# A 4096-step LSTM inside a graph network kernel: the two waits of three VectorE instructions are named in the other order

## What is computed

```python
def step(carry, xp):
    h, c = carry
    gates = xp + h @ W_hh.T
    i, f, g, o = jnp.split(gates, 4, axis=-1)
    c = jax.nn.sigmoid(f) * c + jax.nn.sigmoid(i) * jnp.tanh(g)
    h = jax.nn.sigmoid(o) * jnp.tanh(c)
    return ((h, c), h)
x = x + _L0_gnn_ref(_layernorm(x), adj, ...)   # weights(adj) @ (z W + B)
x = x + _L0_ffn_ref(_layernorm(x)[None], ...)  # the LSTM, then prefix and suffix sums
x = x + _L1_gnn_ref(...)                       # adj @ h / degree
x = x + _L1_ffn_ref(...)                       # causal attention, 8 experts
```

## Time and profile before

| | us |
|---|---|
| time, median of 3 runs (7867.58 to 7874.14) | 7872.52 |
| the profiled execution, its own time | 7870.33 |
| its span, from the first to the last instruction | 7868.3 |
| of that, the stretch of the recurrence (110 to 5915) | 5805 |
| DVE busy over the span | 5390.5 |
| PE busy over the span | 4613.6 |
| ACT busy over the span | 2829.4 |

### The profile page before, as it was taken

The page is one execution under the profiler, slowest core; times in us unless marked ns, Lnnn a source line. Parts: engine busy times, 40 slices in busy tenths (PEclk is TensorE's granted clock), DMA queues, the critical chain, the costliest instruction groups (busy, mean ns, idle before and its releaser), DMA issues. The chain is left out here.

```text
span 7868.3 us, 179097 instructions
## 1 busy us (share of the span) xinstructions
PE 4613.6 (59%) x57632; PEld 3119.7 (40%) x57632; DVE 5390.5 (69%) x30690; ACT 2829.4 (36%) x14714; POOL 217.7 (3%) x504
## 2 busy tenths in 40 slices
PE   4555555555555555555555555555446868788799
PEld 3444444444444444444444444444333421344344
DVE  7666666666666666666666666666646679788544
ACT  3333333333333333333333333333320010488333
POOL 0000000000000000000000000000000020000011
PEclk6555555555555555555555555555558975799799
DMA  1000000000000000000000000000004610000000
GB/s 44 14 12 14 14 12 14 14 13 14 14 14 12 14 14 13 14 14 12 14 14 12 14 14 12 14 14 12 2 2 144 200 48 0 2 1 1 24 4 5
DMA packets 93261, 164.29 MB, mean 21 GB/s; under 512 B 8711, under 2 KB 23087, under 8 KB 92337
## 3 DMA queue, kind: packets, MB, share of 16 engines
q1 hardware_dynamic: 89009, 150.47, 6.1%
q10 hardware_dynamic: 2816, 2.10, 0.1%
q0 software_dynamic: 512, 0.53, 0.0%
HBM read 146.25 MB, written 2.10 MB: 19 GB/s over the span
## 5 line engine op out<-in xcount | busy, mean ns | idle before, releaser
L431 PE MATMUL lstm_gates<-lstm_h_parts,lstm_wrec 128*128 128x1 f16 x36864 | 2074.0, 170 | 2822.8 <-DVE lstm_h_parts L576 2814.6
L431 PEld LDWEIGHTS lstm_gates<-lstm_h_parts,lstm_wrec 128*128 128x128 f16 x36864 | 1615.6, 107 | 3425.4 <-DVE lstm_h_parts L576 3414.3
L487 ACT ACTIVATE lstm_tanhs<-lstm_gates 128x3 f32<-128x3 f32 x4096 | 707.5, 173 | 2726.2 <-PE lstm_gates L431 2726.0
L431 PE MATMUL lstm_gate_o<-lstm_h_parts,lstm_wrec 128*128 128x1 f16 x12288 | 1440.7, 165 | 0.0
L576 DVE SCALAR_TENSOR_TENSOR lstm_h_parts<-lstm_tanh_o,lstm_c_pair 128x1 f16<-128x1 f32 x4096 | 645.5, 158 | 912.8 <-ACT lstm_c_pair L493 912.8
L571 DVE SCALAR_TENSOR_TENSOR lstm_terms<-lstm_tanhs 128x2 f32<-128x2 f32 x4096 | 655.1, 160 | 765.9 <-ACT lstm_tanhs L487 546.1
L595 DVE RECIPROCAL lstm_rec<-lstm_dist 128x52 f32<-128x52 f32 (+1 forms) x2560 | 1171.6, 462 | 4.2 <-issue 4.2
L493 ACT ACTIVATE lstm_c_pair<-lstm_c_pair 128x1 f32<-128x1 f32 x4096 | 639.0, 156 | 951.4 <-DVE lstm_terms L571 951.4
L431 PEld LDWEIGHTS lstm_gate_o<-lstm_h_parts,lstm_wrec 128*128 128x128 f16 x12288 | 961.2, 104 | 0.0
L454 PE MATMUL lstm_acc<-msg,lstm_wt 128*128 128x128 f32 x2048 | 780.9, 488 | 38.2 <-DVE lstm_wt L603 38.2
L582 DVE TENSOR_TENSOR lstm_h_parts<-hid_t,lstm_h_parts 128x1 f16<-128x1 f32 x4096 | 667.5, 163 | 179.9 <-DVE hid_t L578 13.1
(11 more groups left out here) (260 smaller groups left out, 4626.0 us busy)
## 6 DMA issues: line engine op xcount, KB each, us to landing
lstm_ring<-in_adj SPq DMA_DIRECT2D x256, 256.0 KB, 2.7
gnn_ring<-in_adj SPq DMA_DIRECT2D x64, 1024.0 KB, 5.2
w<-in_w SPq DMA_DIRECT2D x2, 1364.0 KB, 9.5
heads_cos<-in_cos SPq DMA_DIRECT2D x8, 256.0 KB, 3.1
heads_sin<-in_sin SPq DMA_DIRECT2D x8, 256.0 KB, 3.5
qs<-heads_q_high SPq DMA_DIRECT2D x64, 32.0 KB, 2.3
out<-x SPq DMA_DIRECT2D x8, 256.0 KB, 2.3
ks<-heads_k_high ACTq DMA_DIRECT2D x16, 64.0 KB, 2.6
```

The lines of the kernel that those rows point to most:

```text
L431: return nc.tensor.matmul(o, wrec[:, w, g, :], h_parts[:, (n - 1) % NH, k:k + 1], start=False, stop=True, skip_group_check=True)
L487: nc.scalar.activation(tanhs[:, 0:3], gates[t % 2][:, i, :], ACT.Tanh, scale=unscale).then_inc(tanhs_ready, 1)
```

## The change

In `step` of DVE the two `wait_ge` lines ahead of L571, L576 and L582 change places. No instruction is added, taken away or moved, and each still waits for the same two semaphores at the same numbers.

```diff
             def step(n):
+                dve.wait_ge(c_kept, n + 1)
                 dve.wait_ge(tanhs_ready, n + 1)
-                dve.wait_ge(c_kept, n + 1)
                 nc.vector.scalar_tensor_tensor(out=terms[:, :], in0=tanhs[:, 0:2], scalar=1.0, in1=tanhs[:, 2:4],
                                                op0=ALU.add, op1=ALU.mult, accum_out=c_twice).then_inc(c_ready, 1)
 
+                dve.wait_ge(tanh_o_ready, n + 1)
                 dve.wait_ge(tanh_c_ready, n + 1)
-                dve.wait_ge(tanh_o_ready, n + 1)
                 nc.vector.scalar_tensor_tensor(out=h_parts[:, n % NH, 0:1], in0=tanh_o[:, :], scalar=1.0,
                                                in1=tanh_c, op0=ALU.add, op1=ALU.mult).then_inc(high_ready, 1)
                 nc.vector.scalar_tensor_tensor(out=T.hid_t[:, n:n + 1], in0=tanh_o[:, :], scalar=1.0,
                                                in1=tanh_c, op0=ALU.add, op1=ALU.mult).then_inc(full_ready, 1)
+                dve.wait_ge(high_ready, n + 2)
                 dve.wait_ge(full_ready, n + 1)
-                dve.wait_ge(high_ready, n + 2)
                 nc.vector.tensor_tensor(h_parts[:, n % NH, 1:2], T.hid_t[:, n:n + 1], h_parts[:, n % NH, 0:1],
                                         ALU.subtract).then_inc(low_ready, 1)
```

## The result

The changed kernel takes 8735.34 us (median of 5 runs, 8731.34 to 8735.83) against 7871.14 us before (5 runs, 7865.7 to 7874.14). The ratio is 1.1097, with a 95% interval of 1.1082 to 1.1113. The forecast was 8780 with a range of 8700 to 8850.

The account below looks back on a forecast made before the run. The prediction took one pass round the ring of PE, ACT and DVE in the recurrence as the bound; 0.211 us of late hops x 4096 = 864 us plus 47 us of stalls made 911, so 8780 us, range 8700 to 8850.

Parts of the forecast that it names:

- The bound: In the recurrence, one pass round a ring of PE, ACT and DVE sets the 1.4175 us step; L571, L576, L582 on it.
- Who holds the late wait: Ahead of L571, L576 and L582, the late wait moves from the instruction to the EVENT_SEMAPHORE in front.
- The price of a late record: At L571 and L576 a hop of 0.107 us instead of 0.0335, so 0.0735 more each, 0.147 per step.
- L155's 0.107: Hop from ACT to DVE behind a late EVENT_SEMAPHORE, read at L155: idle 0.37 less root's 0.23 and one hop 0.0335.
- Predicted 0.064: L582 was to start 0.105 us after L578's end instead of 0.041, 0.064 more per step.
- The stalls: Sequencer hold-ups of 0.356 us, 33 in each of four places ahead of the recurrence's DVE instructions, newly paid: 47 us.
- The Trainium skill's two rules: Instruction fetch mostly hidden: no stall term, 8734 us; semaphore read 50 to 100 ns, three a step: 8484 to 9099 us.
- The third wait is paid: Its rival: L582's wait isn't paid, PE being busy with the high part; 649 us more, 8519 us; 4 in 100.
- One at a time: Rival: behind a late record L578 and the read-out are issued singly, 200 us more, 8980 us; 5 in 100.
- the order doesn't matter: Rival: both waits ahead of each instruction must pass anyway, so the time stays 7870 us; 4 in 100.
- gains: Rival: a late record costs nothing beyond a hop, so L582 gains 31 us, 7840 us; 2 in 100.
- Where the idle time shows: Idle per step: 0.07 more before L571 and L576, L582 from 0.04 to 0.105, ACT before L487 0.21 more, PE's too.

Follow-up runs that it names:

- e3_low: Only the two waits ahead of L582 exchanged, against the kernel before the change: 8132.93 us, ratio 1.0335.
- e4_drop: L576's wait for tanh_o_ready and L582's for high_ready left out, against the kernel before the change: 7825.49 us, ratio 0.9943.
- e5_act: Kernel before the change plus one wait on ScalarE ahead of L493, gate_o_ready named first and late c_ready second: 8147.45 us, ratio 1.0353.

## Why the prediction was right, point by point

- **The bound.** Right: with nothing else changed, every us of delay at L571, L576 and L582 is a us of time (864.2 against 861.0).
- **Who holds the late wait.** Right, and decisive. The text of the change names the early wait first; the built program makes the second one the record in front. The changed profile has L570's records right ahead of L571 and behind the end of L487.
- **The price of a late record.** The mechanism was right, the size a little high. L155's 0.107 was taken for ACT to DVE; it is 0.103 at both places. (At L155 the trace has 0.108 to 0.109 in all five: the record comes as soon, 0.037 to 0.038 after the root, but the reciprocal starts some 5 ns later behind it than L576 does.) The most frequent step went from 1.413 to 1.613, 0.200 and not 0.211: 820 us where the sum had 864. Of the 0.011, 8 ns are the two hops (0.0695 each, not 0.0735), the rest is spread over the other hops. This is the term that was mis-sized. On the profiled execution 8781 was forecast and 8731 measured; 44 of these 50 us are this term, 4 the stalls, and 2 lie outside the steps. The median of the runs lies 4 us above that execution.
- **L582.** Predicted 0.064, read (443.0 - 23.0) / 4034 = 0.104 less 0.041, 0.063.
- **L576 to L578 stay at 0.07 to 0.08, later work stays hidden.** Right: 0.072 to 0.073 outside of stalls, and the later work stays hidden but for the few steps told under the stalls.
- **The stalls.** 47 us forecast. The mean step exceeds the most frequent one by 14.7 ns now (60 us), by 4.2 before (17 us): 43 us. They lie where they were expected: besides the 33 ahead of L582, 31 ahead of L571, 32 at its read-out, 33 ahead of L576, 34 ahead of L578 and 29 at the record of L581. Those make 192 steps, near the 200 forecast, and about 48 us more than the 33 had cost before. What the prediction missed is a place where stalls were paid before: it had L585 and L595 off the path, but in 43 steps, mostly those with a stall ahead of L585 or L595, the delayed DVE work ran into L571 and held it, 5.7 us in all. After the change that is 21 steps and 1.9 us, and so the sum is 43 to 44 and not 48. The lines of the changed kernel's view of L578 show two of the places (who waited: us, times):

```profile
  issue: 7.9, 34
who waited for it (us, times):
  DVE lstm_h_parts L582: 23.0, 62
```

- **The Trainium skill's two rules.** The Trainium skill's "Runtime: NRT & Kernel Launch", section "Instruction fetch mechanics", gave no stall term and 8734. That is the measured time almost to the us, by two errors that cancel: the hops were 44 us cheaper, and the stalls are there, with 43. The Trainium skill's "Advanced Engine Details and Errata", section "Network/Comms", gives 50 to 100 ns for a sequencer's read of a semaphore. The trace agrees: 0.069 more per late record lies inside.
- **The rivals.** The third wait is paid (e3_low). One at a time was wrong: outside of stalls L578 follows L576 by 0.073 as before. That the order doesn't matter, or gains, fell with the result; but the rival's premise, that the record on `high_ready` holds L582 by 0.007, was right, and e4_drop cashes it.
- **Where the idle time shows.** Partly wrong. The prediction put 0.21 more per step of idle time before L487, and before PE's work. ACT's idle before L487 rose by (3288.9 - 2726.0) / 4096 = 0.137 only; the other 0.073 came before L493, which waits for L571. PE's wait for L576 rose by (4007.2 - 3414.3) / 4095 = 0.145, and the delay of L582 comes between its high and its low products. The path and the sum don't rest on this.

## What to carry to other kernels

Before choosing an order of waits, look in the built program at which one the instruction carries: here it is the one written first, so the late wait must be written first. On a chain of short instructions each late wait in a record of its own costs 0.065 to 0.070 us on VectorE, ScalarE and TensorE alike (0.063 where the early record was in the way already), besides the stalls that it brings out, while a record whose semaphore was raised long before is free; that of `high_ready` ahead of L582, raised only 0.06 before the late one, cost 0.007. Best of all is no second wait: where one semaphore implies the other, e4_drop gained 0.6% by leaving the implied ones out.

## What the runs showed of the hardware beyond that

The stalls of DVE's sequencer are regular. In the kernel before, the 33 that delay L582 stand apart in DVE's stream by 256 to 4480 instructions, each time a multiple of 128, and one place in every 128 falls on each of the ten or so instructions of a step in turn, some 30 times each. Each costs 0.35 us when nothing covers it. The same spacing holds after the change in each of the places, and for the 32 stalls of ACT in e5_act. Behind each delayed start, the 33 before and the 192 after, a packet of the instruction queue q14 begins 0.6 to 1.3 us later (mostly 0.66), while such packets lie 13 to 15 us apart on average. The page's part on queues for the changed kernel:

```profile
q8 instruction: 442, 7.24, 0.3%
q14 instruction: 483, 3.95, 0.1%
```

3.95 MB in 483 packets are 8.2 KB each, and 128 instructions of 64 bytes (the size that the Trainium skill's "Perfetto Trace Analysis" gives in "The 4-stage abstract model") are 8192 bytes. So the stall looks like the sequencer turning to ask for its next block of instructions; that is argued from the spacing and the sizes, and no run here took it apart. The places fit a sequencer that hides it while it has run ahead of its engine, which a late record keeps it from doing.
